# Cross attention: the negated maxima as a second accumulating product of 4 rows

## The chip, the cores and the metric

The program runs on one core of a Trainium2 chip. The metric is the device time of one execution in microseconds, the median of three runs. Engines by the profile's names: PE is the tensor engine, PEld its weight loads, DVE the vector engine, ACT the scalar engine, POOL the GpSimd engine, SP the engine that issues most transfers (DMAs).

## The reference

The program is four layers on x of shape (8, 256, 256), each a cross attention or similarity and then a feed-forward part. Three of the layers (0, 2 and 3) have a cross attention with 16 heads of 16 channels over a context of 256 tokens a batch. Layer 0, cut:

```python
q = (x @ Wq).reshape(B, N, HEADS, hd).transpose(0, 2, 1, 3)
k = (context @ Wk).reshape(B, M, HEADS, hd).transpose(0, 2, 1, 3)
v = (context @ Wv).reshape(B, M, HEADS, hd).transpose(0, 2, 1, 3)
scores = jnp.einsum('bhid,bhjd->bhij', q, k) * scale
scores = jnp.where(context_mask[:, None, None, :], scores, max_neg)
attn = jax.nn.softmax(scores, axis=-1)
out = jnp.einsum('bhij,bhjd->bhid', attn, v)
return out.transpose(0, 2, 1, 3).reshape(B, N, DIM) @ Wo
```

Layer 2 has biases and a scale that is an input, layer 3 an output bias; neither has a mask. The softmax takes each row's maximum away before the exponential, and that maximum is what the change is about.

## The kernel before

`xattn_phase` is called three times, once for each of these attentions. It first runs `norm_phase`, under which `fetch` loads the weights and `prepare` fills constants, and then a block in which every engine has its own hand-written order over 8 batches of 16 heads.

Queries and keys are each split in two parts whose sum is the 32-bit value (`khl`, `qhl`: lead and rest). SP writes the parts to DRAM (`send_keys`, `send_queries`) and reads them back as stacks (`stack_keys`, `stack_queries`): for each head 48 rows, lead, lead and rest of the keys (`ks`) against lead, rest and lead of the queries (`qs`), so that one product of 48 rows gives scores of nearly full precision. Even heads lie at partitions 0 to 47, odd heads at 64 to 111. With a mask there is a 49th row (`ROWS_M` = 48 or 49). Three buffers hold the stacks of three batches.

For each batch the scores are made twice. `score` (L478) makes them with queries as rows; DVE takes each head's maxima (`maximum`, L735) into `mx`; PE transposes `mx` once for each half of the heads (`turn_maxima`, L515); ACT copies the result to `mxT` (`put_maxima`, L636). SP then writes `mxT` to DRAM (`send_maxima`, L412) and reads it back into row `MAX_AT` of the query stack (`top_queries`, L418), one row under the 48 or 49; the same row of the key stack holds -1 from the start. `score_T` (L486) makes the scores with keys as rows, with `ROWS_S` = 49 or 50 rows, so that each comes out with its maximum already taken away; ACT takes the exponential straight from the bank (`weights`, L642), and `weigh` (L526) multiplies with the values.

PE's order: `step(b, n)`, n = 0 to 15, has for each of two 128-row halves one `score` of batch b + 1, head n, and one `score_T` of batch b, head n ^ 1. As n and n ^ 1 are of different parity, the two lie in different row halves of the array. Step 0 waits for the stacks of batch b + 1 (`k_in`, `q_in`); steps 0 and 8 wait for the maxima of their half (`max_in`); every step waits for the maximum and the exponential of two steps before. Between the steps of batch b stand: `project_keys` of b + 2 (L454) after step 0, `turn_maxima` after 1 and 10, `weigh` after 2, 5, 9 and 13, `project_queries` (L462) after 3, `turn_out` (L538) after 4 and 6, `project_values` (L472) after 7, `turn_back` (L546) after 8, `output` (L555) after 12. SP's order in a batch: write the second half's maxima, write the keys of b + 2, read the maxima, read the key stacks, write the queries, read the query stacks, write and read the first half's maxima of b + 1. One queue of SP's carries all of them.

Of the kernel before, what the change touches and what calls it, by code (L numbers as in the profile page):

```python
# [14 lines left out]
F32 = mybir.dt.float32  # L15
# [8 lines left out]
P = 128  # L24
# [40 lines left out]
x_rest_put w_lead_put w_rest_put h_lead_put h_rest_put qk_rest on_turned on_put bias_added""".split()  # L65
DMA_SIGNALS = """loaded weights_in even_expert_in odd_expert_in shifted_in stored shared_in
rows_sent scratch_zeroed even_part_in odd_part_in tile_stored quarter0_back quarter1_back quarter2_back
quarter3_back keys_sent queries_sent rows_set even_keys_in odd_keys_in even_queries_in odd_queries_in lower_max_in
upper_max_in lower_max_sent upper_max_sent""".split()


START = 8
# [210 lines left out]
def xattn_phase(c, tag, masked=False, scale=0.25, biased=False, scale_in=False):  # L283
# [15 lines left out]
    k_sent, q_sent, rows_set = c.sig("keys_sent"), c.sig("queries_sent"), c.sig("rows_set")  # L299
    k_in = [c.sig("even_keys_in"), c.sig("odd_keys_in")]  # L300
    q_in = [c.sig("even_queries_in"), c.sig("odd_queries_in")]
    max_sent = [c.sig("lower_max_sent"), c.sig("upper_max_sent")]
    max_in = [c.sig("lower_max_in"), c.sig("upper_max_in")]
    PAIRS, HALF, CH, HPCH, BUFS, SLOTS = HEADS // 2, HEADS // 2, 4, 4, 3, 8
    ROWS_M = 3 * HD + masked
    MAX_AT = ROWS_M
    ROWS_S = ROWS_M + 1
    K_LOADS = 6 + 2 * masked
    with ctx:
        def sb(name, shape, dt=F32):  # L310
            return c.sb("xa_" + name, shape, dt, ctx)
# [4 lines left out]
        bo = sb("bo", [P, 1, D]) if biased else None  # L316
        khl, qhl = sb("khl", [P, 2, KD, S], F32R), sb("qhl", [P, 2, KD, S], F32R)
        ks, qs = sb("ks", [P, BUFS, PAIRS, S], F32R), sb("qs", [P, BUFS, PAIRS, S], F32R)
        consts = sb("consts", [1, 2, PAIRS, S])
        va = sb("v", [P, 2, 2, HEADS, SLOT])  # L320
        mx, mxT = sb("mx", [P, 2, 2, P]), sb("mxT", [P, 2, S], F32R)
        ot, on, onT = sb("ot", [P, 2, CH, S]), sb("on", [P, 2, D]), sb("onT", [P, KD, S])
# [2 lines left out]
        if masked:  # L325
            mask8, mask = sb("mask8", [P, T], U8), sb("mask", [P, T])
            anyk, mbias = sb("anyk", [P, B]), sb("mbias", [1, T], F32R)
        n_loads = 4 + biased + 2 * scale_in + masked
        MSTEPS = 6 if masked else 3 if scale_in else 2

        def fetch(sp):
            for dst, name in ((wq, "wq"), (wk, "wk"), (wv, "wv"), (wo, "wo")):
                sp.dma_start(dst[:], dram[tag + name]).then_inc(loaded.sem, 16)
            if biased:
                sp.dma_start(bo[:], dram[tag + "bo"].partition_broadcast(P)).then_inc(loaded.sem, 16)
            if scale_in:
                sp.dma_start(qcol[:], dram[tag + "qcol"]).then_inc(loaded.sem, 16)
                sp.dma_start(qscale[:], dram[tag + "scale"].partition_broadcast(P)).then_inc(loaded.sem, 16)
            if masked:
                sp.dma_start(mask8[:], dram["mask"].partition_broadcast(P)).then_inc(loaded.sem, 16)  # L340
            sp.wait_ge(*mstep(1))
            for j in range(2):
                for n in range(BUFS):
                    at = 64 * j + MAX_AT
                    sp.dma_start(ks[at:at + 1, n].bitcast(F32), consts[:, 0]).then_inc(rows_set.sem, 16)
                    if masked:
                        sp.dma_start(qs[at - 1:at, n].bitcast(F32), consts[:, 1]).then_inc(rows_set.sem, 16)
            sp.wait_ge(*rows_set(16 * 2 * BUFS * (1 + masked)))

        def prepare(pool):  # L350
            nc.gpsimd.memset(consts[:, 0], -1.0)
            nc.gpsimd.memset(consts[:, 1], 1.0)
            nc.gpsimd.memset(mx[:], 0.0)
            nc.gpsimd.memset(va[:], 1.0).then_inc(mstep.sem, 1)
            pool.wait_ge(*mstep(1))

        norm_phase(c, [(c.x, 0)], fetch=fetch, prepare=prepare)
        rows_set.spent(16 * 2 * BUFS * (1 + masked))
        block = ctx.enter_context(nc.Block(no_gpsimd_drain=True))
        S_BANK, M_BANK, O_BANK, Y_BANK, W_BANK = 0, 3, 5, 6, 7  # L360

# [10 lines left out]
        def _(sp):  # L372
            def send_keys(b):
                sp.wait_ge(*qk_rest(2 * b + 1))
                sp.dma_start(dram["x_keys"][b].rearrange("(a p) t -> p a t", p=P),
                             khl[:].bitcast(F32).rearrange("p a c t -> p (a c) t")).then_inc(k_sent.sem, 16)
# [30 lines left out]
                        sp.dma_start(qs[at:at + HD, b % BUFS].bitcast(F32), parts[part, j]  # L407
                                     ).then_inc(q_in[b % 2].sem, 16)

            def send_maxima(b, half):  # L410
                sp.wait_ge(*topped(2 * b + half + 1))
                sp.dma_start(dram["x_maxima"][b, half], mxT[0:HALF, half].bitcast(F32)).then_inc(max_sent[half].sem, 16)  # L412

            def top_queries(b, half):
                sp.wait_ge(*max_sent[half](16 * b + 16))
                for j in range(2):
                    at = 64 * j + MAX_AT
                    sp.dma_start(qs[at:at + 1, b % BUFS, 4 * half:4 * half + 4].bitcast(F32),  # L418
                                 dram["x_maxima"][b:b + 1, half, 4 * j:4 * j + 4]).then_inc(max_in[half].sem, 16)

            if masked:
                sp.wait_ge(*mstep(MSTEPS))
            send_keys(0)
# [4 lines left out]
            send_queries(1)  # L428
            stack_keys(1)
            stack_queries(1)  # L430
            send_maxima(0, 0)
            top_queries(0, 0)
            for b in range(B):
                send_maxima(b, 1)
                if b + 2 < B:
                    send_keys(b + 2)
                top_queries(b, 1)
                if b + 2 < B:
                    stack_keys(b + 2)
                    send_queries(b + 2)  # L440
                    stack_queries(b + 2)
                if b + 1 < B:
                    send_maxima(b + 1, 0)
                    top_queries(b + 1, 0)
            for half in range(2):
                sp.wait_ge(*max_in[half](32 * B))

        @block.tensor
        def _(pe):
# [33 lines left out]

            def score_T(b, n, h, kt):
                r = 64 * (h % 2)
                ins = nc.tensor.matmul(c.ps[:, S_BANK + (HEADS * b + n) % 3, kt * S:(kt + 1) * S],  # L486
                                       ks[r:r + ROWS_S, b % BUFS, h // 2, kt * P:(kt + 1) * P],
                                       qs[r:r + ROWS_S, b % BUFS, h // 2], start=True, stop=True)
                if kt:
                    ins.then_inc(scored_T.sem, 1)  # L490

            def step(b, n):
                if b + 1 < B:
                    if n == 0:
                        pe.wait_ge(*k_in[(b + 1) % 2](16 * K_LOADS * ((b + 1) // 2 + 1)))
                        pe.wait_ge(*q_in[(b + 1) % 2](16 * 6 * ((b + 1) // 2 + 1)))
                    pe.wait_ge(*max_put(HEADS * (b + 1) + n - 1))
                if b >= 0:
                    if n % HALF == 0:
                        pe.wait_ge(*max_in[n // HALF](32 * b + 32))  # L500
                    pe.wait_ge(*exped(HEADS * b + n - 2))
                for t in range(2):
                    if b + 1 < B:
                        score(b + 1, n, t)
                    if b >= 0:
                        score_T(b, n, n ^ 1, t)
# [98 lines left out]
        def _(act):  # L605
# [26 lines left out]

            def put_maxima(b, half):
                act.wait_ge(*max_turned(2 * b + half + 1))
                act.wait_ge(*max_in[half](32 * b))
                nc.scalar.copy(mxT[0:HALF, half], c.ps[0:HALF, Y_BANK, 0:S]).then_inc(topped.sem, 1)  # L636

            def weights(b, n):
                h = n ^ 1
# [51 lines left out]
        def _(dve):  # L691
# [12 lines left out]
            if scale_in:  # L704
                step.mark(nc.vector.tensor_scalar(qcol[:], qcol[:], qscale[:, 0:1], None, ALU.mult))
                step.link(dve, nc.vector.tensor_scalar(wq[:], wq[:], qscale[:, 0:1], None, ALU.mult))
            else:
                step.link(dve, nc.vector.tensor_scalar(wq[:], wq[:], scale, None, ALU.mult))
            assert step.n == MSTEPS

            def rest_keys(b):
# [16 lines left out]
                ins.then_inc(qk_rest.sem, 1)  # L728

            def maximum(b, h):  # L730
                half, col = h // HALF, 4 * (h % 2) + h % HALF // 2
                dve.wait_ge(*scored(HEADS * b + h + 1))
                if h % HALF == 0:
                    dve.wait_ge(*max_turned(2 * (b - 1) + half + 1))
                nc.vector.tensor_reduce(mx[:, half, :, col],  # L735
                                        c.ps[:, M_BANK + h % 2].rearrange("p (t n) -> p t n", t=2), AX_X, ALU.max
                                        ).then_inc(max_put.sem, 1)
# [48 lines left out]
    for par in range(2):  # L786
        k_in[par].spent(16 * K_LOADS * (B // 2))
        q_in[par].spent(16 * 6 * (B // 2))
        max_sent[par].spent(16 * B)
        max_in[par].spent(32 * B)  # L790
    for sgn, n in ((qk_proj, 2), (qk_put, 2), (qk_rest, 2), (v_proj, 1), (v_put, 1), (scored, HEADS),
                   (max_put, HEADS), (max_turned, 2), (topped, 2), (scored_T, HEADS), (exped, HEADS), (weighed, CH),
                   (o_put, CH), (o_turned, 2), (inverted, 2), (o_normed, 2), (on_turned, 1), (on_put, 1), (y_done, 1),
# [1585 lines left out]
def _layouts(inp):  # L2379
# [5 lines left out]
    o["mask"] = a["mask_BxS2_bf1"].reshape(1, T).view(np.uint8)  # L2385
    o["ident"] = np.eye(P, dtype=f4)
    o["ctxT"][KC[1], 1] = 1.0
    for tag, src in (("L0x_", "L0_xattn_"), ("L2x_", "L2_xattn_"), ("L3x_", "L3_xattn_")):
        for name in ("Wq", "Wk", "Wv", "Wo"):
            o[tag + name.lower()] = _chunked(a[src + name])  # L2390
# [30 lines left out]
```

## Time and profile before

| what | us |
|---|---|
| median of 3 runs (lowest, highest) | 3147.41 (3137.94, 3162.08) |
| the profiled execution | 3133.37 |
| its span, first to last instruction | 3131.4 |
| PE busy, in the span | 2382.8 (76%) |
| DVE busy | 1304.5 (42%) |
| ACT busy | 1069.4 (34%) |
| mean granted clock of PE | 0.859 |

The profile is of one execution. The page gives busy times, the costliest groups of instructions and what ended the idle time before them; the trace behind it can be asked for a timeline, for who waited for whom, and for stretches. A group's line has its source line, engine, operation, what it writes from what, its shape and its count; then busy time, mean ns of one, and the idle time of the engine ahead of it with what ended most of it. "issue" is idle time for which no semaphore is to blame. A granted clock of 1.0 is 2.4 GHz, 0.5 is 1.2 GHz.

### The profile page before, as it was taken

The page shows a single profiled execution, that of the slowest core. Times are in us where ns is not written, and L with a number is a line of the kernel's source. Part 1 is how long each engine was busy: PE and PEld are TensorE (multiplying, and loading weights), DVE is VectorE, ACT ScalarE, POOL GpSimd, SP SyncE. Part 2 cuts the span into 40 slices and gives each one's busy share as a digit, 9 for nine tenths or more (in the row PEclk, how much of TensorE's full clock was granted, in tenths as well). Part 3 has the DMA queues.
Part 4 walks back from the last instruction along what each step waited for, and adds up shares of the span by engine and source line. Part 5 has one row for each costly group of instructions (what it writes and reads, how often), then busy time and mean ns, then how long its engine had stood idle before and what let it go on. Part 6 is the DMA issues. An engine that isn't in the chain of part 4 may idle for free. (4 is left out here: it accounts for less than half of the span.)

```text
span 3131.4 us, 43799 instructions
## 1 busy us (share of the span) xinstructions
PE 2382.8 (76%) x13240; PEld 1710.2 (55%) x13241; DVE 1304.5 (42%) x2813; ACT 1069.4 (34%) x2518; POOL 624.4 (20%) x622
## 2 busy tenths in 40 slices
PE   3788389349798788798694776988998267846998
PEld 2455179224465574365573554557997144525887
DVE  3444400368665417755414444200000434446554
ACT  1345123223354413355421444213443124432332
POOL 1000300216411325611322000310000500022343
PEclk9778689669799899899796888988999669878999
DMA  6542232100000000000004542103220364300000
GB/s 189 87 87 52 79 125 108 41 24 0 10 0 17 28 5 20 9 0 11 33 1 83 97 82 57 67 29 119 84 96 30 83 102 82 66 13 21 20 25 32
DMA packets 119680, 165.60 MB, mean 53 GB/s; under 512 B 14657, under 2 KB 106676, under 8 KB 114452
## 3 DMA queue, kind: packets, MB, share of 16 engines
q1 hardware_dynamic: 114964, 151.62, 19.6%
q0 software_dynamic: 4608, 12.59, 1.2%
q8 instruction: 61, 1.00, 0.1%
q14 instruction: 47, 0.39, 0.0%
HBM read 114.43 MB, written 47.32 MB: 52 GB/s over the span
## 5 line engine op out<-in xcount | busy, mean ns | idle before, releaser
L735 DVE TENSOR_REDUCE xa_mx<-ps 128x2 f32<-128x512 f32 x384 | 257.8, 690 | 375.0 <-PE ps L478 368.9
L642 ACT ACTIVATE xn_tok<-ps 128x512 f32<-128x512 f32 x384 | 227.8, 599 | 312.9 <-PE ps L486 312.2
L478 PE MATMUL ps<-xa_ks,xa_qs 48*128 48x256 f32 (+1 forms) x768 | 204.8, 368 | 110.8 <-DMA xa_qs<-x_maxima 85.7
L255 PE MATMUL ps<-ident,ln_row 128*128 128x128 f32 x288 | 67.7, 397 | 242.6 <-DVE ln_row L225 240.1
L478 PEld LDWEIGHTS ps<-xa_ks,xa_qs 48*128 48x128 f32 (+1 forms) x768 | 131.0, 219 | 215.6 <-issue 161.5
L232 POOL TENSOR_TENSOR ln_rstd<-ln_var,pow_half 128x16 f32<-128x16 f32 x10 | 29.2, 2915 | 1026.4 <-DVE ln_var L214 1026.4
L1218 PE MATMUL ps<-ex_tiles,ex_w 128*128 x1792 | 213.4, 278 | 7.7 <-issue 4.1
L1218 PEld LDWEIGHTS ps<-ex_tiles,ex_w 128*128 128x128 f32 x1792 | 212.8, 195 | 11.1 <-issue 8.3
L1224 PE MATMUL ps<-ex_w,ex_h 128*128 128x256 f32 x896 | 202.7, 379 | 0.0
L255 PEld LDWEIGHTS ps<-ident,ln_row 128*128 128x128 f32 x288 | 46.0, 197 | 265.0 <-DVE ln_row L225 258.6
L486 PE MATMUL ps<-xa_qs,xa_ks 49*128 49x256 f32 (+1 forms) x768 | 189.5, 347 | 1.3 <-DMA xa_qs<-x_maxima 0.8
L1738 PE MATMUL ps<-lp_wqkv,lp_hs 128*128 128x512 f32 x384 | 176.1, 610 | 4.7 <-ACT lp_hs L1782 4.3
L1224 PEld LDWEIGHTS ps<-ex_w,ex_h 128*128 128x128 f32 x896 | 166.0, 190 | 20.2
L1238 ACT ACTIVATE ex_h<-ps,ex_b 128x128 f32<-128x128 f32 x296 | 108.6, 367 | 152.3 <-PE ps L1218 131.8
L1276 POOL DMA_INDIRECT xn_tok<-rows_out,rows_back x32 | 31.2, 975 | 551.9 <-DMA rows_out<-ex_tiles 542.7
L1254 DVE TENSOR_TENSOR ex_tiles<-ps,ex_b 128x256 f32 x37 | 15.7, 424 | 277.5 <-PE ps L1224 270.9
L486 PEld LDWEIGHTS ps<-xa_qs,xa_ks 49*128 49x128 f32 (+1 forms) x768 | 118.2, 203 | 9.8 <-ACT xn_tok L642 6.9
L1525 POOL TENSOR_TENSOR ge_hl<-ge_h,ge_hh 128x512 fp32r<-128x512 f32 x64 | 82.6, 1290 | 195.0 <-ACT ge_hh L1514 195.0
L1738 PEld LDWEIGHTS ps<-lp_wqkv,lp_hs 128*128 128x128 f32 x384 | 72.1, 194 | 89.8 <-issue 84.8
L526 PE MATMUL ps<-xn_tok,xa_v 128*32 128x256 f32 x1536 | 109.7, 406 | 4.3 <-ACT xn_tok L642 4.3
L1436 PE MATMUL ps<-ge_xh,ge_wh 128*128 128x512 f32 x256 | 81.8, 401 | 40.8 <-PEq L1303 24.5
L1988 ACT ACTIVATE lw_p<-ps,lw_nm 128x128 f32<-128x128 f32 (+1 forms) x256 | 106.0, 424 | 15.0 <-DVE lw_nm L2039 15.0
(294 smaller groups left out, 5243.8 us busy)
## 6 DMA issues: line engine op xcount, KB each, us to landing
xa_ks<-x_keys SPq DMA_DIRECT2D x144, 128.0 KB
xa_qs<-x_queries SPq DMA_DIRECT2D x144, 128.0 KB, 4.7
ex_w<-in_L0f_w_dram SPq DMA_DIRECT2D x16, 1024.0 KB
ex_w<-in_L2f_w_dram SPq DMA_DIRECT2D x16, 1024.0 KB
x_keys<-xa_khl SPq DMA_DIRECT2D x24, 512.0 KB, 3.0
x_queries<-xa_qhl SPq DMA_DIRECT2D x24, 512.0 KB, 5.5
di_rows<-rows_in SPq DMA_DIRECT2D x16, 512.0 KB, 3.8
rows_out<-ex_tiles SPq DMA_DIRECT2D x62, 128.0 KB, 1.7
```

Of the source, the lines that this page charges most:

```text
L255: ins = nc.tensor.transpose(c.ps[:, s, k * P:(k + 1) * P], xs[:, s, k * P:(k + 1) * P], c.ident[:])
L478: ins = nc.tensor.matmul(c.ps[:, M_BANK + h % 2, qt * S:(qt + 1) * S], qs[r:r + ROWS_M, b % BUFS, n, qt * P:(qt + 1) * P], ks[r:r + ROWS_M ...
L486: ins = nc.tensor.matmul(c.ps[:, S_BANK + (HEADS * b + n) % 3, kt * S:(kt + 1) * S], ks[r:r + ROWS_S, b % BUFS, h // 2, kt * P:(kt + 1) * ...
L526: ins = nc.tensor.matmul(c.ps[j * SLOT:(j + 1) * SLOT, O_BANK, 0:S], va[:, b % 2, kt, h], pT[:, h % SLOTS, kt], start=(kt == 0), stop=(kt ...
L642: nc.scalar.activation(pT[:, h % SLOTS].rearrange("p k q -> p (k q)"), c.ps[:, S_BANK + (HEADS * b + n) % 3], ACT.Exp).then_inc(exped.sem, 1)
L735: nc.vector.tensor_reduce(mx[:, half, :, col], c.ps[:, M_BANK + h % 2].rearrange("p (t n) -> p t n", t=2), AX_X, ALU.max).then_inc(max_put ...
L1218: ins = nc.tensor.matmul(c.ps[:, f % 4, 0:P], w1[:, par, k, f * P:(f + 1) * P], tile_of(n)[:, k], start=(k == 0), stop=(k == KD - 1))
L1224: ins = nc.tensor.matmul(c.ps[:, 4, 0:D], h[:, f], w2[:, par, f], start=(f == 0), stop=(f == FC - 1))
L1238: nc.scalar.activation(h[:, f], c.ps[:, f % 4, 0:P], ACT.Relu if first else ACT.Silu, bias=0.0 if first else b1[:, par, f:f + 1]).then_inc ...
L1525: nc.gpsimd.tensor_tensor(hl[:, g % 2], h[:, g % 2], hh[:, g % 2].bitcast(F32), ALU.subtract).then_inc(h_rest.sem, 1)
L1738: ins = nc.tensor.matmul(c.ps[:, 3 * tt + n, :], hs[:, k, tt * P:(tt + 1) * P], wqkv[:, k, n * INNER:(n + 1) * INNER], start=(k == 0), sto ...
L1988: ins = nc.scalar.activation(pr[:, h % AHEAD, lo:hi], c.ps[:, 1 + h % AHEAD, lo:hi], ACT.Exp, bias=nm[:, h, n:n + 1], accum_out=rs[:, h, n ...
```

## The change

The row of maxima leaves the query stack, and the row of -1 the key stack. `send_maxima` and `top_queries` with their four semaphores go, and so do their DRAM buffer and the transfers that set the -1 rows. `score_T` becomes two products that accumulate in one bank: the old one with 48 or 49 rows (start), and a second one of 4 rows (`PER_HALF`) that adds `take_max`, a matrix with -1 in the row of the head's own maximum, times 4 rows of `mxT`. To have the maxima at the partitions of the heads, `maximum` writes to column 64 * (h % 2) + ... of `mx`, and `put_maxima` copies all 128 partitions. `take_max` comes from a new input `less` (128 x 4 x 128), loaded with the weights and copied by DVE ahead of the first projection. The query and key transfers of batch b + 2 keep their order and lose the maxima's transfers between them. Steps 0 and 8 of PE wait for `topped` (ACT's copy) in place of `max_in`, and `put_maxima` waits for the transposed scores of the batch before in place of `max_in`.

```diff
-    MAX_AT = ROWS_M
-    ROWS_S = ROWS_M + 1
+    PER_HALF = PAIRS // 2
...
-        consts = sb("consts", [1, 2, PAIRS, S])
+        consts = sb("consts", [1, PAIRS, S])
+        less, take_max = sb("less", [P, PER_HALF, P]), sb("take_max", [P, PER_HALF, P], F32R)
...
-            sp.wait_ge(*mstep(1))
-            for j in range(2):
-                for n in range(BUFS):
-                    at = 64 * j + MAX_AT
-                    sp.dma_start(ks[at:at + 1, n].bitcast(F32), consts[:, 0]).then_inc(rows_set.sem, 16)
-                    if masked:
-                        sp.dma_start(qs[at - 1:at, n].bitcast(F32), consts[:, 1]).then_inc(rows_set.sem, 16)
-            sp.wait_ge(*rows_set(16 * 2 * BUFS * (1 + masked)))
+            sp.dma_start(less[:], dram["less"]).then_inc(loaded.sem, 16)
+            if masked:
+                sp.wait_ge(*mstep(1))
+                for j in range(2):
+                    for n in range(BUFS):
+                        at = 64 * j + 3 * HD
+                        sp.dma_start(qs[at:at + 1, n].bitcast(F32), consts[:]).then_inc(rows_set.sem, 16)
+                sp.wait_ge(*rows_set(16 * 2 * BUFS))
...
-            send_maxima(0, 0)
-            top_queries(0, 0)
-            for b in range(B):
-                send_maxima(b, 1)
-                if b + 2 < B:
-                    send_keys(b + 2)
-                top_queries(b, 1)
-                if b + 2 < B:
-                    stack_keys(b + 2)
-                    send_queries(b + 2)
-                    stack_queries(b + 2)
-                if b + 1 < B:
-                    send_maxima(b + 1, 0)
-                    top_queries(b + 1, 0)
-            for half in range(2):
-                sp.wait_ge(*max_in[half](32 * B))
+            for b in range(2, B):
+                send_keys(b)
+                stack_keys(b)
+                send_queries(b)
+                stack_queries(b)
...
+                nc.tensor.matmul(c.ps[:, S_BANK + (HEADS * b + n) % 3, kt * S:(kt + 1) * S],
+                                 ks[r:r + ROWS_M, b % BUFS, h // 2, kt * P:(kt + 1) * P],
+                                       qs[r:r + ROWS_M, b % BUFS, h // 2], start=True, stop=False)
                 ins = nc.tensor.matmul(c.ps[:, S_BANK + (HEADS * b + n) % 3, kt * S:(kt + 1) * S],
-                                       ks[r:r + ROWS_S, b % BUFS, h // 2, kt * P:(kt + 1) * P],
-                                       qs[r:r + ROWS_S, b % BUFS, h // 2], start=True, stop=True)
+                                       take_max[r:r + PER_HALF, h % HALF // 2], mxT[r:r + PER_HALF, h // HALF],
+                                       start=False, stop=True)
...
-                        pe.wait_ge(*max_in[n // HALF](32 * b + 32))
+                        pe.wait_ge(*topped(2 * b + n // HALF + 1))
...
-                act.wait_ge(*max_in[half](32 * b))
-                nc.scalar.copy(mxT[0:HALF, half], c.ps[0:HALF, Y_BANK, 0:S]).then_inc(topped.sem, 1)
+                act.wait_ge(*scored_T(HEADS * (b - 1) + HALF * (half + 1)))
+                nc.scalar.copy(mxT[:, half], c.ps[:, Y_BANK, 0:S]).then_inc(topped.sem, 1)
...
+            step.link(dve, nc.vector.tensor_copy(take_max[:], less[:]))
...
-                half, col = h // HALF, 4 * (h % 2) + h % HALF // 2
+                half, col = h // HALF, 64 * (h % 2) + h % HALF // 2
...
+    o["less"] = np.zeros((P, 4, P), f4)
+    for n in range(4):
+        o["less"][[n, 64 + n], n] = -1.0
```

## Rows read from the trace of the kernel before

**Rows 1.** The page's costliest groups; columns as described above, times in us, mean in ns

```profile
L735 DVE TENSOR_REDUCE xa_mx<-ps 128x2 f32<-128x512 f32 x384 | 257.8, 690 | 375.0 <-PE ps L478 368.9
L642 ACT ACTIVATE xn_tok<-ps 128x512 f32<-128x512 f32 x384 | 227.8, 599 | 312.9 <-PE ps L486 312.2
```

**Rows 2.** The instructions of L418: who waited for them, us and times

```profile
  PE ps L478: 85.7, 20
```

**Rows 3.** Stretches (us): length, busy PE, PEld, DVE, ACT, POOL, clock, DMA share, GB/s

```profile
1719.40:1933.20 213.80, 169.43 (x1302) 109.04 (x1304) 96.01 (x165) 98.52 (x206) 0.00 (x0) 0.89 0.42 76
92.60:313.80 221.20, 180.85 (x1298) 115.31 (x1298) 95.50 (x159) 97.95 (x200) 0.00 (x0) 0.83 0.39 74
2530.00:2753.00 223.00, 175.06 (x1302) 112.31 (x1303) 94.97 (x159) 97.37 (x200) 0.00 (x0) 0.85 0.40 73
75.60:88.00 12.40, 10.51 (x33) 7.55 (x33) 9.56 (x15) 0.00 (x0) 0.00 (x0) 0.50 1.09 166
```

**Rows 4.** Timeline of SP, second attention: start, length of all (us), line, operation, count

```profile
1797.87 2.67 SPq L407 DMA_DIRECT2D xa_qs<-x_queries  x6
1800.59 0.33 SPq L412 DMA_DIRECT2D x_maxima<-xa_mxT  x1
1805.54 0.52 SPq L418 DMA_DIRECT2D xa_qs<-x_maxima  x2
```

**Rows 5.** Timeline of PE, products of steps 10 and 11 and between; idle time in brackets

```profile
1796.10 1.07 PE L526 MATMUL ps<-xn_tok,xa_v 128*32 128x256 f32 x16
1797.10 0.38 PE L478 MATMUL ps<-xa_ks,xa_qs 48*128 48x256 f32 x1
...
1797.33 0.28 PE L478 MATMUL ps<-xa_ks,xa_qs 48*128 48x256 f32 x1
...
1797.54 0.44 PE L515 MATMUL ps<-ident,xa_mx 128*128 128x128 f32 x2
1797.90 0.38 PE L478 MATMUL ps<-xa_ks,xa_qs 48*128 48x256 f32 x1
```

**Rows 6.** Timeline of PE's weight loads, the same stretch

```profile
1797.53 0.20 PEld L515 LDWEIGHTS ps<-ident,xa_mx 128*128 128x128 f32 x2
```

**Rows 7.** Timeline of PE's weight loads in the local transformer: products of 1 and 128 rows

```profile
1097.19 0.19 PEld L2194 LDWEIGHTS ps<-lf_w_lead,lf_h_lead 128*128 128x128 f32 x1 [0.33 <-issue]
...
1097.42 0.19 PEld L2194 LDWEIGHTS ps<-lf_w_less,lf_h_lead 128*128 128x128 f32 x1
1097.54 0.19 PEld L2194 LDWEIGHTS ps<-lf_w_lead,lf_h_lead 128*128 128x128 f32 x1
```

**Rows 8.** Timeline of PE: a turn, a step, a projection, a step

```profile
1791.74 0.63 PE L538 MATMUL ps<-ident,xa_ot 128*128 128x128 f32 x4 [0.84 <-DVE xa_on L746]
1792.30 0.38 PE L478 MATMUL ps<-xa_ks,xa_qs 48*128 48x256 f32 x1
...
1792.73 1.99 PE L472 MATMUL ps<-xa_wv,ctx_T 128*128 128x256 f32 x8
1794.65 0.38 PE L478 MATMUL ps<-xa_ks,xa_qs 48*128 48x256 f32 x1
```

**Rows 9.** Timeline of PE: first product of step 0, batches 2 and 3

```profile
1779.54 0.35 PE L478 MATMUL ps<-xa_ks,xa_qs 48*128 48x256 f32 x1 [1.96 <-DMA xa_qs<-x_maxima]
...
1807.47 0.55 PE L478 MATMUL ps<-xa_ks,xa_qs 48*128 48x256 f32 x1 [3.95 <-DMA xa_qs<-x_maxima]
```

**Rows 10.** Timeline of PE: step 3 and the projection of queries behind it

```profile
1784.14 0.38 PE L478 MATMUL ps<-xa_ks,xa_qs 48*128 48x256 f32 x1
...
1786.02 0.48 PE L462 MATMUL ps<-xn_T,xa_wq 128*128 128x256 f32 x1 [1.38 <-DVE xa_khl L717]
```

**Rows 11.** Timeline of PE after a long wait: a projection, a step, a turn

```profile
1749.37 0.55 PE L478 MATMUL ps<-xa_ks,xa_qs 48*128 48x256 f32 x1 [7.96 <-DMA xa_qs<-x_maxima]
...
1750.10 3.78 PE L454 MATMUL ps<-ctx_T,xa_wk 128*128 128x256 f32 x8
1753.81 0.58 PE L478 MATMUL ps<-xa_ks,xa_qs 48*128 48x256 f32 x1
...
1754.53 0.64 PE L515 MATMUL ps<-ident,xa_mx 128*128 128x128 f32 x2
```

More of the change, by code:

```diff
@@ L67 @@
 rows_sent scratch_zeroed even_part_in odd_part_in tile_stored quarter0_back quarter1_back quarter2_back
-quarter3_back keys_sent queries_sent rows_set even_keys_in odd_keys_in even_queries_in odd_queries_in lower_max_in
-upper_max_in lower_max_sent upper_max_sent""".split()
+quarter3_back keys_sent queries_sent rows_set
+even_keys_in odd_keys_in even_queries_in odd_queries_in""".split()
 START = 8
@@ L301, in xattn_phase @@
     q_in = [c.sig("even_queries_in"), c.sig("odd_queries_in")]
-    max_sent = [c.sig("lower_max_sent"), c.sig("upper_max_sent")]
-    max_in = [c.sig("lower_max_in"), c.sig("upper_max_in")]
     PAIRS, HALF, CH, HPCH, BUFS, SLOTS = HEADS // 2, HEADS // 2, 4, 4, 3, 8
     ROWS_M = 3 * HD + masked
-    MAX_AT = ROWS_M
-    ROWS_S = ROWS_M + 1
+    PER_HALF = PAIRS // 2
     K_LOADS = 6 + 2 * masked
@@ L327, in xattn_phase @@
             anyk, mbias = sb("anyk", [P, B]), sb("mbias", [1, T], F32R)
-        n_loads = 4 + biased + 2 * scale_in + masked
-        MSTEPS = 6 if masked else 3 if scale_in else 2
+        n_loads = 5 + biased + 2 * scale_in + masked
+        MSTEPS = 7 if masked else 4 if scale_in else 3
         def fetch(sp):
@@ L340, in fetch @@
                 sp.dma_start(mask8[:], dram["mask"].partition_broadcast(P)).then_inc(loaded.sem, 16)
-            sp.wait_ge(*mstep(1))
-            for j in range(2):
-                for n in range(BUFS):
-                    at = 64 * j + MAX_AT
-                    sp.dma_start(ks[at:at + 1, n].bitcast(F32), consts[:, 0]).then_inc(rows_set.sem, 16)
-                    if masked:
-                        sp.dma_start(qs[at - 1:at, n].bitcast(F32), consts[:, 1]).then_inc(rows_set.sem, 16)
-            sp.wait_ge(*rows_set(16 * 2 * BUFS * (1 + masked)))
+            sp.dma_start(less[:], dram["less"]).then_inc(loaded.sem, 16)
[6 more added lines that the diff above has]
+                sp.wait_ge(*rows_set(16 * 2 * BUFS))
         def prepare(pool):
-            nc.gpsimd.memset(consts[:, 0], -1.0)
-            nc.gpsimd.memset(consts[:, 1], 1.0)
+            nc.gpsimd.memset(consts[:], 1.0)
             nc.gpsimd.memset(mx[:], 0.0)
@@ L357, in xattn_phase @@
         norm_phase(c, [(c.x, 0)], fetch=fetch, prepare=prepare)
-        rows_set.spent(16 * 2 * BUFS * (1 + masked))
+        rows_set.spent(16 * 2 * BUFS * masked)
         block = ctx.enter_context(nc.Block(no_gpsimd_drain=True))
@@ L408, in stack_queries @@
                                      ).then_inc(q_in[b % 2].sem, 16)
[L410 to L419, printed above, removed]
             if masked:
@@ L788, in xattn_phase @@
         q_in[par].spent(16 * 6 * (B // 2))
-        max_sent[par].spent(16 * B)
-        max_in[par].spent(32 * B)
     for sgn, n in ((qk_proj, 2), (qk_put, 2), (qk_rest, 2), (v_proj, 1), (v_put, 1), (scored, HEADS),
@@ L2416 @@
         dram[name] = nc.dram_tensor(name, (B, 2 * D, S), _mybir.dt.float32, kind="Internal").ap()
-    dram["x_maxima"] = nc.dram_tensor("x_maxima", (B, 2, HEADS // 2, S), _mybir.dt.float32, kind="Internal").ap()
     _program(nc, dram, STAGES)
```

## The prediction, made before the changed kernel was run

> **What bounds the kernel now.** I read the page first, for the share of the three cross attentions and who waits for whom in them; then the waits behind the transfer that the change removes; then the three attentions as stretches; and last the timelines of one batch on SP, PE and PE's weight loads. In the costliest groups the vector engine's maxima and the scalar engine's exponentials are idle for longer than they are busy, and both wait for the score products [rows 1]. So inside the attention PE's own order of work, or whatever PE waits for, sets the pace. PE's largest single wait there is the one the change aims at: 85.7 us in 20 waits, 4.3 us each, for the row of maxima that comes back from DRAM [rows 2]. The three attentions, from the first transposed score to the last weighing, take 221.2, 213.8 and 223.0 us, 658.0 together, of a span of 3131.4 [rows 3]; everything else is left as it was. One full batch in the second attention starts at 1779.54 and the next at 1807.47, after a wait of 3.95: 27.9 us, of which 24.0 are not that wait [rows 9].
>
> **What is removed.** Not the whole wait goes. PE's step 0 also needs the stacked keys and queries of the next batch. The queue shows the six query stacks issued until 1800.54, the maxima's write right behind them at 1800.59, and the read only at 1805.54, when the write had landed [rows 4]. The stacks before it on the same queue are there by about then, and the product starts at 1807.47 [rows 9]. So the transfers left would let a batch start about 1.9 us earlier; more of the wait can go only if PE's own work grows into it. Of the 24 batches, 20 have such a wait [rows 2].
>
> **What is added.** In every step n, 384 in all, each of two key halves gets a second product of 4 rows behind the one of 48 or 49, and the next batch's scores stand between. The order becomes: pair (L478 with L486, side by side in rows 0 and 64 of the array), 4-row product, pair, 4-row product. What does one 4-row product cost? The trace has two answers, far apart.
>
> Lower bound: products of 256 columns of one shape, one after the other, have their weights loaded under the product before. The loads follow each other by 0.12 us [rows 7]. By that a step grows by 0.23.
>
> Upper bound: where the height of the product changes, nothing is loaded ahead. After the 1-row products of L2191 the load engine is idle 0.33, with "issue" as the reason, before the first 128-row load [rows 7]. After a step the load of L515 (128 rows) starts at 1797.53 [rows 6], 0.20 after the last pair at 1797.33, and its step, begun at 1797.10, has held PE for 0.43 [rows 5]. That is two pairs of which the second cost 0.12, so one pair with a change of shape behind it holds PE for 0.31. The trace shows such a gap at changes between 1, 48 to 50 (or 64) and 128 rows, and none between 48 and 49, which run side by side. Whether 4 rows are to 48 as 48 are to 49, or as 1 is to 128, no row says. I take the upper price: the nearest height in the trace below 48 is the single row, and products of one row pay for the change. Then each step is four units with a change behind each: 4 x 0.31 = 1.25 us, against 0.43.
>
> The Trainium skill (TensorEngine Tiling, Key Properties) says the same of the mechanism: "Changing tiling mode (not just tile) drains the TensorE", and lists 64-row and 32-row tiles as different modes; the gaps [rows 6, 7] agree with it, for other pairs of shapes. By that rule the upper price holds; without it the lower one would be as open.
>
> **The sum, all at 2.4 GHz.** A full batch on PE: 16 steps of 1.25 = 20.0. Four projections and outputs of 1.92 (L472: 1792.73 to 1794.65) = 7.7, two turns and one back-turn of 0.57 (L538: 1791.74 to 1792.30) = 1.7 [rows 8]; four weighings of 1.00 (1796.10 to 1797.10) = 4.0, two turns of maxima of 0.37 = 0.7 [rows 5]. One wait for the vector engine stays: L462 starts 1.88 after step 3 starts [rows 10]; the second pair, on whose scores it depends, now starts two units and a load in (0.73) and not at 0.23, 0.5 later, so 1.88 + 0.5 - 1.25 = 1.1. Together 35.2. The other waits vanish under the longer steps, and so does the wait for the transfers: they allow 27.9 - 1.9 = 26 us, plus the 3 us by which steps 0 to 3 delay the keys, which is less than 35.2. There are 15 full batches (528). The first of each attention has no weighing, turns or output of an earlier one: 35.2 - 1.0 - 1.7 - 1.9 = 30.6 (92). The seventh has no projections for a later one, nor the wait: 35.2 - 3.8 - 1.1 = 30.3 (91). The last has only L486's side, but its order 48, 4, 48, 4 has the same four units: 20.0 + 1.9 + 4.0 + 1.7 + 0.4 = 28.0, and 0.6 for the last exponential [rows 1], which waits for the second 4-row product: 28.6 (86). Sum 797 against 658: +139.
>
> Small parts: the first batch of each attention loses a wait too; of at most 4.3 each [rows 2] I take half, -6. The new copy of 128x512 on the vector engine, ahead of the first projection, costs as much as a pass over 512 elements, 0.69 [rows 1], three times: +2. Free: the 256 KB more of loads and the fewer constants and row transfers, which lie under the norm ahead of the attention, and the maxima's turn, which moves as many columns as before. So +135.
>
> **The clock.** Granted clock is 0.83, 0.89 and 0.85 in the three attentions [rows 3], so PE ran at 1.2 GHz for 34, 22 and 30% of the time. Such a stretch followed a long wait: after the 7.96 us before 1749.37 a projection takes 3.78 instead of 1.99 and a step holds PE for 0.72 instead of 0.43 [rows 11, 8]; a unit is then about 0.50, a step 2.0. Without waits for transfers much of this should go. But a PE that loads and drains does little work: the stretch of untransposed scores alone, 33 products in 12.4 us, ran at 0.50 throughout [rows 3]. I take half the share of before, 15%; work is then slower by about 1.7, so 797 becomes 797 / (1 - 0.41 x 0.15) = 849: +52.
>
> Total 3131.4 + 135 + 52 = 3318; the execution lies 2 above its span, and the median of the timed runs 14 above the profiled execution: **3334 us**, 6% slower.
>
> **Rivals.**
> - *The 4-row product is cheap* (0.12, same kind as the 48 rows). A full batch is 24.0 + 16 x 0.23 = 27.7, near what the transfers allow; first 27, seventh 22.5, last 17.5; sum 616, which gives 3131 - 42 - 4 + 16 = 3101, faster. For it: the waits for the maxima [rows 2]. Against it: every change of height that the rows show [rows 5 to 7]. It decides if a 4-row product holds PE for under 0.2 us. Chance 0.09.
> - *Only one of the two changes drains* (say, into 4 rows but not back). A step is 1.25 - 0.4 = 0.85, a full batch 28.8, about the 28 to 30 that it takes with its waits now; sum about 655, time 3145, no change. Chance 0.07.
> - *The full price, and the clock falls to 1.2 GHz half of the time*, since pairs and drains are thin work as in the stretch at 0.50 [rows 3]: 797 / (1 - 0.41 x 0.5) = 1003, time 3488. Chance 0.14. At 2.4 GHz throughout it would be 3282.
> - My forecast, the full price with 0 to a third of the time at 1.2 GHz: 0.70.
>
> **Range and chances.** 3235 to 3465 leaves out the two cheap cases and the worst of the clock. Faster or slower by over 1% (31 us) is about what a measurement of this kernel can tell. Faster 0.08, same 0.07, slower 0.85.
>
> **What would show it.** In the profile after: a step with its two 4-row products holds PE for 1.2 to 1.3 us at 2.4 GHz; the weight load of each 4-row product starts about 0.2 after the pair before it, not with it; no wait of PE at step 0 for transfers, above all none for stacks over 1 us; an interval between batches of 34 to 42 us; 768 more products, and the maxima's and exponentials' idle time larger, not smaller. Wrong if the 4-row load starts within 0.02 of the pair, or if PE still waits for stacks at step 0. The clock share is the weakest number.

## The result, and the profile after

The changed kernel takes 3785.11 us (median of 3, 3784.48 to 3785.79), the kernel before 3147.41: a ratio of 1.202, interval 1.1945 to 1.2094. It is slower, as forecast, but by 638 us and not by 187; the range ended at 3465. The profiled execution's span is 3783.0 us at a mean granted clock of 0.745, against 3131.4 at 0.859.

The page's costliest groups of the changed kernel, in the columns of [rows 1]. L714 and L620 are the maxima and the exponentials (L735 and L642 before), L453 the scores, L461 the transposed scores, L464 the new product of 4 rows:

```profile
L714 DVE TENSOR_REDUCE xa_mx<-ps 128x2 f32<-128x512 f32 x384 | 263.9, 693 | 897.4 <-PE ps L453 897.4
L620 ACT ACTIVATE xn_tok<-ps 128x512 f32<-128x512 f32 x384 | 229.3, 597 | 912.9 <-PE ps L464 912.9
L453 PE MATMUL ps<-xa_ks,xa_qs 48*128 48x256 f32 (+1 forms) x768 | 397.5, 538 | 31.6 <-issue 20.8
L461 PE MATMUL ps<-xa_qs,xa_ks 48*128 48x256 f32 (+1 forms) x768 | 420.9, 548 | 0.0
L464 PE MATMUL ps<-xa_mxT,xa_take_max 4*128 4x256 f32 x768 | 418.8, 545 | 0.0
```

DVE and ACT do the same work in the same time as in [rows 1], but wait for PE 897 and 913 us instead of 375 and 313. A score product takes 538 ns where it took 368. PE no longer waits for maxima from DRAM, the 85.7 us of [rows 2]; it waits for itself.

The three attentions, from the first transposed score to the last weighing, in the columns of [rows 3]:

```profile
90.60:518.80 428.20, 421.89 (x1555) 237.24 (x1557) 97.83 (x159) 102.85 (x200) 0.00 (x0) 0.54 0.20 38
1945.80:2375.50 429.70, 423.75 (x1555) 238.46 (x1557) 98.57 (x165) 103.86 (x206) 0.00 (x0) 0.54 0.20 37
2975.00:3403.00 428.00, 422.05 (x1556) 237.65 (x1558) 97.45 (x159) 102.24 (x200) 0.00 (x0) 0.54 0.20 37
```

Together 1285.9 us against 658.0 [rows 3]: 628 of the 652 us by which the span grew. (These stretches begin 1.4 us behind the first transposed score, in the runs below 0.1 to 2.3 us behind it; at most 7 us in all are missed by it.) The other 24 lie outside these stretches, where little but the loading and copying of `take_max` was changed; that part is 2497 us here, 2473 in the kernel before, and between 2452 and 2494 in the runs below, so the 24 can't be told from noise. The granted clock in the attentions is 0.54, that is, PE ran at 1.2 GHz for 92% of their time, though it was busy for 1267.7 of the 1285.9 us. (Busy includes the time in which a change of height holds the array.)

One step at 2.4 GHz, from the timeline of PE, and then the weight loads of the same step:

```profile
2023.49 0.38 PE L453 MATMUL ps<-xa_ks,xa_qs 48*128 48x256 f32 x1
...
2023.81 0.38 PE L464 MATMUL ps<-xa_mxT,xa_take_max 4*128 4x256 f32 x1
2024.12 0.38 PE L453 MATMUL ps<-xa_ks,xa_qs 48*128 48x256 f32 x1
...
2024.43 0.38 PE L464 MATMUL ps<-xa_mxT,xa_take_max 4*128 4x256 f32 x1
2024.74 0.66 PE L524 MATMUL ps<-ident,xa_on 128*128 128x128 f32 x4
```

```profile
2023.81 0.18 PEld L464 LDWEIGHTS ps<-xa_mxT,xa_take_max 4*128 4x128 f32 x1
2024.12 0.18 PEld L453 LDWEIGHTS ps<-xa_ks,xa_qs 48*128 48x128 f32 x1
```

The four units are there, each 0.31 to 0.32 us, 1.25 in all (2023.49 to 2024.74), against 0.43 for the step of [rows 5]. Each load starts with its product and none ahead of it. (The scores of L461 start with those of L453, beside them, and are left out here.) Half a step at 1.2 GHz, where nearly all of them run:

```profile
2100.24 0.58 PE L453 MATMUL ps<-xa_ks,xa_qs 48*128 48x256 f32 x1
...
2100.76 0.57 PE L464 MATMUL ps<-xa_mxT,xa_take_max 4*128 4x256 f32 x1
2101.26 0.58 PE L453 MATMUL ps<-xa_ks,xa_qs 48*128 48x256 f32 x1
```

1.02 us for two units, 2.03 for a step. Four stretches of one batch show when the clock rose and fell. They are the end of the projection of values (L447, 128 rows), the steps after it, a stretch soon after, and the rest up to the next such projection:

```profile
2022.00:2023.50 1.50, 1.50 (x6) 0.68 (x4) 0.00 (x0) 0.00 (x0) 0.00 (x0) 0.50 0.73 85
2025.00:2026.50 1.50, 1.50 (x10) 0.90 (x8) 0.35 (x2) 0.92 (x2) 0.00 (x0) 1.00 0.00 0
2028.00:2029.50 1.50, 1.50 (x9) 0.86 (x5) 0.00 (x0) 0.00 (x0) 0.00 (x0) 0.50 0.00 0
2028.00:2077.50 49.50, 48.62 (x172) 27.27 (x168) 11.91 (x20) 10.76 (x22) 0.00 (x0) 0.50 0.22 45
```

PE was busy without a break through the first three. It came to 2.4 GHz behind eight products of 128 rows, and fell back over a few steps and weighings, with no wait before the fall. The other three projections of the batch, in the last stretch, did not raise it.

### The profile page after: what moved, and what is told of

It is laid out like the page before. It is cut to its first block and busy times, and to the rows that moved or that the text cites. A ratio compares the mean times of both kernels' runs of the same rounds, so it can differ in the third digit from the quotient of the medians.

```text
span 3783.0 us, 45168 instructions
## 1 busy us (share of the span) xinstructions
PE 3150.3 (83%) x14008; PEld 2102.2 (56%) x14009; DVE 1311.3 (35%) x2816; ACT 1084.2 (29%) x2518; POOL 619.1 (16%) x619
## 5 line engine op out<-in xcount | busy, mean ns | idle before, releaser
L714 DVE TENSOR_REDUCE xa_mx<-ps 128x2 f32<-128x512 f32 x384 | 263.9, 693 | 897.4 <-PE ps L453 897.4
L620 ACT ACTIVATE xn_tok<-ps 128x512 f32<-128x512 f32 x384 | 229.3, 597 | 912.9 <-PE ps L464 912.9
L453 PE MATMUL ps<-xa_ks,xa_qs 48*128 48x256 f32 (+1 forms) x768 | 397.5, 538 | 31.6 <-issue 20.8
L461 PE MATMUL ps<-xa_qs,xa_ks 48*128 48x256 f32 (+1 forms) x768 | 420.9, 548 | 0.0
L464 PE MATMUL ps<-xa_mxT,xa_take_max 4*128 4x256 f32 x768 | 418.8, 545 | 0.0
L453 PEld LDWEIGHTS ps<-xa_ks,xa_qs 48*128 48x128 f32 (+1 forms) x768 | 202.2, 272 | 266.3 <-issue 228.6
L464 PEld LDWEIGHTS ps<-xa_mxT,xa_take_max 4*128 4x128 f32 x768 | 204.3, 266 | 160.2 <-issue 145.2
L461 PEld LDWEIGHTS ps<-xa_qs,xa_ks 48*128 48x128 f32 (+1 forms) x768 | 206.8, 269 | 31.1 <-issue 28.1
L504 PE MATMUL ps<-xn_tok,xa_v 128*32 128x256 f32 x1536 | 178.2, 611 | 2.1 <-ACT xn_tok L620 2.1
```

Source lines behind the costliest of these rows:

```text
L453: ins = nc.tensor.matmul(c.ps[:, M_BANK + h % 2, qt * S:(qt + 1) * S], qs[r:r + ROWS_M, b % BUFS, n, qt * P:(qt + 1) * P], ks[r:r + ROWS_M ...
L504: ins = nc.tensor.matmul(c.ps[j * SLOT:(j + 1) * SLOT, O_BANK, 0:S], va[:, b % 2, kt, h], pT[:, h % SLOTS, kt], start=(kt == 0), stop=(kt ...
L620: nc.scalar.activation(pT[:, h % SLOTS].rearrange("p k q -> p (k q)"), c.ps[:, S_BANK + (HEADS * b + n) % 3], ACT.Exp).then_inc(exped.sem, 1)
L714: nc.vector.tensor_reduce(mx[:, half, :, col], c.ps[:, M_BANK + h % 2].rearrange("p (t n) -> p t n", t=2), AX_X, ALU.max).then_inc(max_put ...
```

## The experiments

The theory from the prediction was that a product of 4 rows next to products of 48 changes the height of the array's tile, that no weights are loaded ahead over such a change, and that each of the four changes in a step costs about 0.2 us. Its rivals: the second product costs by itself, whatever its height; the new waits cost. After the result there was a second question: why the clock fell to 0.54 although the waits for transfers were gone.

**64 rows instead of 4** (e1_rows64). One edit to the changed kernel:

```diff
-                                       take_max[r:r + PER_HALF, h % HALF // 2], mxT[r:r + PER_HALF, h // HALF],
+                                       take_max[r:r + 64, h % HALF // 2], mxT[r:r + 64, h // HALF],
```

> The changed kernel with one edit: the second product takes 64 rows of the same two tiles instead of 4; the other 60 rows are zeros on both sides, so the result is the same. Theory 1 (height): what costs is the change between products of 48 and of 4 rows, which lets no weights be loaded ahead; 64 rows run as 48 do, so a step holds PE for 0.65 to 0.7 us instead of 1.25 at 2.4 GHz, and the attentions fall from 428 us each to about 205: 3100 us in all (3060 to 3160). Theory 2 (product): the second product costs because it accumulates on the bank of the one before it, or simply by its number; its height changes nothing: 3785. Theory 3 (waits): the new waits at steps 0 and 8 cost the time: 3785 too.

Measured: 3096.62 us, 0.983 of the kernel before (interval 0.979 to 0.987). The timeline of PE and the three attentions as stretches:

```profile
1803.07 0.38 PE L453 MATMUL ps<-xa_ks,xa_qs 48*128 48x256 f32 x1
...
1803.30 0.28 PE L464 MATMUL ps<-xa_mxT,xa_take_max 64*128 64x256 f32 x1
1803.42 0.28 PE L461 MATMUL ps<-xa_qs,xa_ks 48*128 48x256 f32 x1
1803.54 0.28 PE L464 MATMUL ps<-xa_mxT,xa_take_max 64*128 64x256 f32 x1
1803.74 0.44 PE L493 MATMUL ps<-ident,xa_mx 128*128 128x128 f32 x2
```

```profile
87.90:299.10 211.20, 180.98 (x1557) 126.83 (x1558) 95.50 (x159) 99.41 (x200) 0.00 (x0) 0.96 0.41 76
1714.80:1921.80 207.00, 181.81 (x1556) 127.34 (x1558) 96.14 (x165) 99.74 (x206) 0.00 (x0) 0.97 0.42 77
2516.80:2724.10 207.30, 181.82 (x1558) 127.44 (x1558) 95.15 (x159) 98.79 (x200) 0.00 (x0) 0.96 0.42 77
```

The same number of products, the same waits, 60 more rows of zeros: a step holds PE for 0.67 us and not 1.25 (1803.07 to 1803.74), the products of one row half follow each other by 0.12, and 688 us are gone. That rules out the product as such and the waits.

**The 4-row product alone** (e2_before_plus4), in the kernel before with its transfers:

```diff
-                                       qs[r:r + ROWS_S, b % BUFS, h // 2], start=True, stop=True)
+                                       qs[r:r + ROWS_S, b % BUFS, h // 2], start=True, stop=False)
+                ins = nc.tensor.matmul(c.ps[:, S_BANK + (HEADS * b + n) % 3, kt * S:(kt + 1) * S],
+                                       nil[r:r + 4, 0:P], nil[r:r + 4, :], start=False, stop=True)
```

> The kernel before, with its transfers and waits as they are, and one addition: behind each transposed score product (49 or 50 rows) an accumulating product of 4 rows whose operands are zeros, so that the result stays. Theories 1 and 2: nearly all of the loss comes with this product alone: 3750 to 3830. Theory 3 (the waits of the change): 3150 to 3250.

Measured: 3789.06 us, a ratio of 1.205 (1.198 to 1.212), at clocks of 0.54, 0.55 and 0.53 in the attentions. The whole loss comes with this product. The waits for the maxima, 85.7 us in the kernel before, are down to 12.3 here: most of what the change dropped hides behind the longer steps.

**Two changes of height in a step instead of four** (e3_two_changes). The products are the same; the second 4-row product goes first in its half of the bank:

```diff
+            def less_max(b, n, h, kt):
+                r = 64 * (h % 2)
+                nc.tensor.matmul(c.ps[:, S_BANK + (HEADS * b + n) % 3, kt * S:(kt + 1) * S],
+                                 take_max[r:r + PER_HALF, h % HALF // 2], mxT[r:r + PER_HALF, h // HALF],
+                                 start=(kt == 1), stop=(kt == 0))
...
                     if b >= 0:
                         score_T(b, n, n ^ 1, t)
+                        if t == 0:
+                            less_max(b, n, n ^ 1, 0)
+                            less_max(b, n, n ^ 1, 1)
```

> The changed kernel with the same products in another order: pair, 4-row product, 4-row product, pair, so that the height changes twice in a step and not four times. Theory 1: at 2.4 GHz a step holds PE for 1.05 us (two units of 0.31, and 0.12 + 0.31 for the two 4-row products) or 0.86 between two steps, at 1.2 GHz about 1.7 and 1.3 instead of 2.03; with the clock as in the changed kernel some 100 to 150 us less: 3650 (3600 to 3700), less still if PE's clock recovers. Theory 2 (cost by product, whatever the order): 3785.

Measured: 3412.33 us, a ratio of 1.084 (1.078 to 1.089). Timeline of PE, and the second attention as a stretch:

```profile
1903.01 0.38 PE L453 MATMUL ps<-xa_ks,xa_qs 48*128 48x256 f32 x1
...
1903.33 0.50 PE L469 MATMUL ps<-xa_mxT,xa_take_max 4*128 4x256 f32 x2
1903.75 0.38 PE L453 MATMUL ps<-xa_ks,xa_qs 48*128 48x256 f32 x1
...
1904.07 2.21 PE L447 MATMUL ps<-xa_wv,ctx_T 128*128 128x256 f32 x5
```

```profile
1808.10:2107.60 299.50, 287.89 (x1555) 178.55 (x1558) 98.31 (x165) 102.78 (x206) 0.00 (x0) 0.78 0.30 53
```

A step takes 1.06 us at 2.4 GHz, as expected (1.05). The time fell by 373 and not by 100 to 150, because the clock rose too, to 0.75, 0.78 and 0.70 in the three attentions. The number that I had given held for the step and missed the clock, as the prediction had. So the clock too depends on the changes of height: the products are the same as in the changed kernel, only their order differs.

**32 and 33 rows** (e7_rows32, e8_rows33): the edit of the first experiment with 32 and with 33 in place of 64.

> The second product takes 32 rows, 28 of them zeros. If the border that makes a change of height lies between 32 and 33 rows, this costs as 4 rows do: 3770 to 3800. If it is nearness to 48 rows that counts, the cost is in between: 3300 to 3600.

> One row more than the run with 32: the second product takes 33 rows, 29 of them zeros. With the border between 32 and 33 this is as fast as with 64 rows: 3080 to 3120. If nearness counts, it is as the run with 32 rows, 3300 or more.

Measured: 3744.99 us with 32 rows (ratio 1.199, 1.192 to 1.205), 3094.53 with 33 (0.990, 0.988 to 0.992). The second attention of the first, and of the second:

```profile
1933.70:2360.80 427.10, 421.15 (x1555) 236.63 (x1557) 98.49 (x165) 103.85 (x206) 0.00 (x0) 0.54 0.20 37
```

```profile
1729.80:1946.00 216.20, 191.54 (x1556) 133.42 (x1558) 96.19 (x165) 99.61 (x206) 0.00 (x0) 0.91 0.42 74
```

One row of zeros more makes the whole kernel 650 us faster. So what counts is not how near the heights are but on which side of 32 they lie. (With 32 rows the time is 25 us under the range that I had given.) The clock with 32 rows is 0.53, 0.54 and 0.56 in the three attentions, as with 4: 28 more rows of zeros did nothing for it. The Trainium skill (TensorEngine Tiling (Array Packing), Available Configurations) lists tiles of 32, 64 and 128 rows; the two runs agree with a border of 32.

**Why the clock fell: three times the scores** (e4_after_scores3x). The changed kernel with each of the untransposed score products made three times:

```diff
-                ins = nc.tensor.matmul(c.ps[:, M_BANK + h % 2, qt * S:(qt + 1) * S],
+                for _ in range(3):
+                    ins = nc.tensor.matmul(c.ps[:, M_BANK + h % 2, qt * S:(qt + 1) * S],
...
```

> The changed kernel with more work for PE: each untransposed score product (L453) is made three times in place of once, into the same place. At 2.4 GHz that adds 0.46 us to a step (1.71), at 1.2 GHz about 0.9 (2.9). Theory A (the clock fell because the steps are thin work): with the filling the clock rises again, the batch takes about 43 us instead of 58 and the whole 3460, less than the changed kernel in spite of 1536 more products. Theory B (the clock doesn't follow how full the steps are): a batch of 72 us and 4100.

Measured: 3954.23 us in the profiled execution and 4022.86 in the only other one. In the second attention of the first:

```profile
1991.00:2482.80 491.80, 485.86 (x1998) 309.45 (x2001) 98.56 (x165) 103.79 (x206) 0.00 (x0) 0.58 0.18 33
```

The clock hardly moved, from 0.54 to 0.58, though PE makes twice as many products of 48 rows in a step. Theory A as I had put it falls: more products of that height, with the four changes kept, do not bring the clock back. The time is between the two that were given, nearer to theory B's 4100.

**The second product with all 128 rows** (e6_rows128), so that each step keeps its changes of height but the array has more rows at work. Only 8 of the 128 rows hold maxima; the others are zeros on both sides:

```diff
-                                       take_max[r:r + PER_HALF, h % HALF // 2], mxT[r:r + PER_HALF, h // HALF],
+                                       take_max[:, 4 * (h % 2) + h % HALF // 2], mxT[:, h // HALF],
...
-    o["less"] = np.zeros((P, 4, P), f4)
+    o["less"] = np.zeros((P, 8, P), f4)
     for n in range(4):
-        o["less"][[n, 64 + n], n] = -1.0
+        o["less"][n, n] = o["less"][64 + n, 4 + n] = -1.0
```

> The changed kernel with a second product of all 128 rows, 124 of them zero weights over real maxima: as many changes of height as with 4 rows (64 to 128 and back), but far more of the array at work. Both theories of the clock give a step of 1.25 us at 2.4 GHz and 2.03 at 1.2. Theory A (the clock fell because 4 rows are little work for the array): it recovers, at 0.9 or more a batch takes 36 to 38 us: 3300 to 3350. Theory C (it fell because of the changes of height, whatever the rows): 3760 to 3810 at a clock of 0.54 in the attentions.

Measured: 3394.67 us, a ratio of 1.087 (1.080 to 1.093). Timeline of PE over one step, and the second attention as a stretch:

```profile
1883.63 0.38 PE L453 MATMUL ps<-xa_ks,xa_qs 48*128 48x256 f32 x1
...
1883.94 0.39 PE L464 MATMUL ps<-xa_mxT,xa_take_max 128*128 128x256 f32 x1
1884.26 0.38 PE L453 MATMUL ps<-xa_ks,xa_qs 48*128 48x256 f32 x1
...
1884.57 0.38 PE L464 MATMUL ps<-xa_mxT,xa_take_max 128*128 128x256 f32 x1
1884.88 0.38 PE L453 MATMUL ps<-xa_ks,xa_qs 48*128 48x256 f32 x1
```

```profile
1822.90:2115.30 292.40, 285.33 (x1555) 173.88 (x1557) 98.50 (x165) 103.16 (x206) 0.00 (x0) 0.86 0.31 55
```

A step with another step behind it takes the same 1.25 us (1883.63 to 1884.88), with the same count of products; only where other products of 128 rows follow is one change saved. Yet the clock is 0.81, 0.86 and 0.80 instead of 0.54, and the attentions take 912 us instead of 1286. The time is still above the 3300 to 3350 of theory A, as the clock stayed under 0.9. So changes of height alone do not force the clock of the changed kernel: theory C is refuted, and the height of the second product counts.

It is not the whole cause either. Four runs stand beside the changed kernel (0.54). The same products with two changes of height in a step instead of four gave 0.70 to 0.78. The same changes with 128 rows gave 0.80 to 0.86. The same changes with 32 rows gave 0.53 to 0.56, and with twice as many products of 48 rows 0.58 or 0.59. The last makes 2.1 products of 48 rows in a microsecond of its attentions and the run with two changes 1.7, at the higher clock, so neither the rows at work nor the products in a microsecond put these runs in order. The 4-row product and its changes of height together took the clock down; which measure of the work the chip takes is open.

The run with 33 rows had 0.92, 0.91 and 0.93 in its attentions, and the one with 64 rows 0.96 or 0.97. That difference is not shown to be one of the rows: the profiled execution with 33 rows was the slowest of its nine (3115.95 against a median of 3094.53), and over the whole program the two have the same median clock, 0.877 and 0.878.

**What the transfers were worth** (e5_no_second). The changed kernel with one product for the transposed scores; the maximum is not taken away, and the exponential is of a hundredth of the score.

```diff
-                nc.tensor.matmul(c.ps[:, S_BANK + (HEADS * b + n) % 3, kt * S:(kt + 1) * S],
-                                 ks[r:r + ROWS_M, b % BUFS, h // 2, kt * P:(kt + 1) * P],
-                                       qs[r:r + ROWS_M, b % BUFS, h // 2], start=True, stop=False)
...
-                                       take_max[r:r + PER_HALF, h % HALF // 2], mxT[r:r + PER_HALF, h // HALF],
-                                       start=False, stop=True)
+                                       ks[r:r + ROWS_M, b % BUFS, h // 2, kt * P:(kt + 1) * P],
+                                       qs[r:r + ROWS_M, b % BUFS, h // 2], start=True, stop=True)
...
-                                     c.ps[:, S_BANK + (HEADS * b + n) % 3], ACT.Exp).then_inc(exped.sem, 1)
+                                     c.ps[:, S_BANK + (HEADS * b + n) % 3], ACT.Exp, scale=0.01).then_inc(exped.sem, 1)
```

> What the transfers alone were worth. The changed kernel without its second product: the transposed scores are one product of 48 or 49 rows, the maxima are made, turned and copied but not taken away, and the exponential is taken of a hundredth of the score so that it stays finite; the rest of the work is the same. By the prediction's lower case the batch is then bound by the stacks, 26 us after 27.9, first 26, seventh 19.5, last 15.5: about 3060 (3040 to 3085). Rival: another wait takes the place of the one removed, and the time is that of the run with 64 rows or more: 3095 to 3145.

Measured: 3080.94 us, a ratio of 0.986 (0.981 to 0.990). What PE still waited for (us, times, longest), first here and then with the 64-row product:

```profile
PE ps L453 <- DMA xa_qs<-x_queries: 49.2, 17, 6.3
```

```profile
PE ps L453 <- DMA xa_qs<-x_queries: 29.3, 11, 6.8
```

The second attention of this run:

```profile
1709.50:1918.70 209.20, 174.34 (x1298) 111.62 (x1299) 96.10 (x165) 98.83 (x206) 0.00 (x0) 0.87 0.43 76
```

The wait moves from the maxima to the query stacks, as the prediction had said, and 49 of the 86 us stay. Without the transfers' waits, and with no second product, the clock is 0.87 in all three attentions, where it was 0.83, 0.89 and 0.85 before: the gain in clock that I had hoped for from the shorter waits is small. The 64-row product with its 0.23 us a step costs little beside this run, 0.4% by the runs with 33 rows (beside it) and with 64 rows (below, against the same 3125 us of the kernel before). It fills 20 us of the wait for the stacks, and the clock is 0.96 instead of 0.87.

**The 64-row product with the transfers kept** (e9_before_plus64), beside the 64-row version of the change again (e10_rows64_again). The first is the edit of e2_before_plus4 with 64 rows:

```diff
-                                       nil[r:r + 4, 0:P], nil[r:r + 4, :], start=False, stop=True)
+                                       nil[r:r + 64, 0:P], nil[r:r + 64, :], start=False, stop=True)
```

> The kernel before, transfers of the maxima and all, with a second product of zeros as in the earlier run, but of 64 rows: no change of height, and more of the array at work. If the gain of the 64-row version lies in the transfers that it drops, this one keeps the waits of 86 us for them and adds 0.23 us to each step: 3150 to 3190. If it lies in the clock that the added rows hold up, this one has most of it: 3090 to 3120, at a clock of 0.92 or more in the attentions.

> The changed kernel with a second product of 64 rows once more, beside the run above on the same chip: 1.5 to 2% faster than the kernel before.

Measured: 3159.68 us (ratio 1.011, 1.008 to 1.014) and 3093.48 us (0.989, 0.986 to 0.992). What PE waited for in the first, and its second attention:

```profile
PE ps L479 <- DMA xa_qs<-x_maxima: 71.3, 21, 8.1
```

```profile
1746.90:1971.40 224.50, 189.27 (x1558) 131.71 (x1558) 96.25 (x165) 99.29 (x206) 0.00 (x0) 0.92 0.41 72
```

With equal products, dropping the transfers is worth 66 us. The clock does rise with the added rows (0.92, 0.92 and 0.90, where it was 0.83, 0.89 and 0.85), but that alone does not pay for them: this run is 35 us slower than the kernel before. The gain of the 64-row version is that of the transfers less the product's cost. Against the kernel before it is 1.1% in this comparison, less than the 1.5 to 2% that I expected, and 1.7% in the first one, whose intervals just overlap. With 33 rows it was 1.0%. These are the fastest versions with the whole computation that I ran, and they can't be told apart.

## Why the prediction was right in direction and wrong in size

- **The price of the 4-row product**, where I chose between 0.12 and 0.31 us, was right: 0.31 at 2.4 GHz, a step of 1.25. The load comes 0.32 after the pair's, not with it. I had written about 0.2, read from a pair whose own weights were loaded 0.11 before its product; here none are. The rival "cheap product" is refuted for 4 rows and is what happens at 33 and more: its sum gave 3101, and the 64-row version took 3097 and 3093.
- **Only one of the changes drains**: refuted, both units take 0.31. Its sum of 655 was off: 15 x 28.8 + 3 x (24.2 + 23.9 + 22.2) is 643, or 3129 us in all, which is no change either.
- **The waits**: right but for the first batch of each attention. No wait for maxima is left; three waits for query stacks are, 5.3 us together and 2.4 the longest, one at step 0 of each first batch, where I had said none over 1 us. After the first batch PE is the bound.
- **The sum at 2.4 GHz**, 35.2 us for a full batch and 797 for the attentions, was not reached by the changed kernel, since it hardly ran at that clock. The 128-row run bears it out. Two of its batches in the second attention ran at 2.4 GHz throughout and took 34.1 us each, with some changes saved before other products of 128 rows:

```profile
1875.75:1943.99 68.24, 66.11 (x417) 41.42 (x417) 28.45 (x49) 26.82 (x54) 0.00 (x0) 1.00 0.44 78
```

- **The clock** is the step that failed: "I take half the share of before, 15%". It was 92%. The formula of that part held; with 0.92 it gives 797 / (1 - 0.41 x 0.92) = 1280 us, and 1285.9 were measured, 437 more than the 849 of the forecast. That is nearly all of the 451 us between 3334 and 3785.11. The rest nearly cancels: outside the attentions the span grew by 24 where I had -4, and the median lies on the profiled execution and not 14 above it. A full batch took 55.4 to 58.0 us, not 34 to 42. I had reasoned that the long waits made the clock fall and that without them it would rise; they did go, and it fell from 0.83, 0.89 and 0.85 to 0.54 with PE busy. The rival with the clock at 1.2 GHz half of the time had the direction right, with a chance of 0.14, and its 3488 was still 297 too low. The row behind it, the stretch of untransposed scores at 0.50 [rows 3], was the nearer guide, though PE was busy for only 10.51 of its 12.4 us. What the runs show in place of my step: with a second product of 4 or 32 rows and four changes of height in a step, PE stays at 1.2 GHz for some nine tenths of the time without any wait; fewer changes or a second product of 128 rows bring part of the clock back. Why, is open.

## What to carry to other kernels

Before adding a short product between taller ones, look at which side of 32 rows each lies, and pad the short one with zero rows to its neighbours' side: here that turned a loss of 20% into a gain of 1.0 to 1.7%. A product of 128 rows between those of 48 cost its changes of height too (a step of 1.25 us); where between 64 and 128 rows the next border lies, no run here shows. A price for PE worked out at 2.4 GHz must be accompanied by the question of whether the new sequence keeps that clock, even where PE has no waits; here the clock added 489 us to the sum at 2.4 GHz (1285.9 against 797). A wait of PE that a change removes leaves room for PE work, but find the next wait on the same step first: of 86 us, 49 came back as a wait for the stacks.

## What the runs showed of the hardware that I had not expected

- PE was granted 1.2 GHz for 92% of 1286 us in which it was busy for 1268. At the same changes of height the clock was 0.54 with a second product of 4 rows, 0.53 to 0.56 with 32 rows and 0.80 to 0.86 with 128, nearly all of them zeros. With half the changes and the 4-row products kept it was 0.70 to 0.78. Without them it was 0.91 to 0.93 with 33 rows and 0.95 to 0.97 with 64.
- Three score products in place of one, all of 48 rows, raised it only from 0.54 to 0.58 or 0.59.
- The border between 32 and 33 rows is sharp in the time of a whole kernel: 3745 against 3095 us.
